# Rotation tables of the second to fourth layer made by GpSimd in place of VectorE

## The chip, the cores and the metric
One Trainium2 chip, one core, one launch of the whole program. The metric is the device time in microseconds, the median of several executions. The core has TensorE (PE, matmuls and transposes), VectorE (DVE), ScalarE (ACT), GpSimd (POOL) and SyncE (SP, which here only issues DMAs). Each engine works through its own list of instructions in order, and engines wait for one another on semaphores.

## The reference, cut to what matters
The input is 8 sequences of 256 tokens of 512 numbers. Four parts follow one another, each added to its input after a layer norm: a small four-layer stack, a gated feed-forward network whose weights are scaled by a low-rank product, an attention, and the same feed-forward network again. The change touches only the first part. Each of its four layers does, with 64 channels:

```
y = silu(layernorm(h, l1w, l1b))
r = abs(phazor); p = tanh(r) * exp(1j * angle(phazor))
prog = p ** arange(L)                      # a decaying rotation, per channel
y = real(causal convolution of y with prog + last_conv * prog * p)
h = h + y * scl
h = h + W2 @ silu(W1 @ layernorm(h) + b1) + b2
```

The convolution with powers of p is a linear recurrence z[t] = p z[t-1] + y[t].

## The kernel before, in words
The kernel is in three phases; the first holds the stack and the first feed-forward network, beside preparations for the attention. The tokens are cut into four blocks of 512 (`NBLK` = 4), and each block passes the stack as a stack of its own, s = 0 to 3; s = 0 is called the lead, because the feed-forward network of block 0 can begin only when it is through. Then the network runs over blocks 0 to 3, 14 weight chunks each (`gate`, `up`, `down`, matmuls in the helper of line 837), and stacks 1 to 3 are worked off between its matmuls on TensorE.

In a layer the phases of the recurrence are taken out by a rotation: the input is multiplied by cos and sin of the angle times t (`ur` on VectorE, line 1765, and `ui` on GpSimd, line 1270), two real scans with the decay rho run over time (`zr`, `zi`, line 1776), and the results are multiplied by the same tables again (`pr`, line 1780, `pi`, line 1273), possibly summed (`prs`, line 1784) and taken through a matmul (`conv`). Each norm in a stack has the steps `sq` (squares, ScalarE), `h` (VectorE), `var` (TensorE), `eps` (VectorE, line 1751), `rstd` (the inverse root, GpSimd, line 1262), `rtr` (TensorE) and `yn` (VectorE, line 1757).

The tables are `rot`, cos and sin for 4 layers and 256 times (`cosT`, `sinT`). They are made by doubling in eight levels (`LEVELS` = 8): level k makes the columns n to 2n, n = 2^k, from the columns 0 to n by a rotation through the angle of n steps. That angle's cos and sin (`turn`) are squared up level by level on GpSimd (`turns`, lines 1239 to 1245; the semaphore `rot_done` counts them). Layer 0's table is made on VectorE level by level (`tab0`, `dve_table`, lines 1631 and 1633). The tables of layers 1 to 3 are made on VectorE too (`tabs`, `dve_tables`): levels 0 to 4 for the three layers together in three instructions each (lines 1649, 1656, 1658), levels 5 to 7 (`TAB_EACH` = 5) layer by layer in two instructions each (lines 1649, 1652). Each instruction counts up `tabs_dve`; `ui` and `ur` of layers 1 to 3 wait for the count `TABS[l]`, and the first two silus of the network's gate (line 1317) for `TABS["all"]`, since the scratch memory `tab` is the memory of `gate`.

The order of every engine's list in phase 1 comes from a greedy planner (`Steps.ordered`) that runs when the program is built. A step has an engine, a cost in us, the steps it comes after and an urgency. Each result is ready for others 0.12 us after its end (`LAG`; 0.25 for TensorE, none between two TensorE steps). The planner always places the ready step that ranks first by

```
late = urgent > 0 and at < patient and e in need and at + us > need[e] + 0.1
rank = (late, at, urgent, number[k])
```

where `at` is the earliest start, `number` the place in which the step was added, and `need[e]` the earliest expected start on that engine of a step of the lead (urgency 0) all of whose predecessors have a known time. The steps at issue are added in this loop, after the tile norms (`ln`, and `inv` on GpSimd, cost 1.7, urgency 2 in blocks 1 and later):

```
for k in range(LEVELS):
    o.add(("turn", k, 0), "pool", 1.0 if k else 0.2, ..., 1)
    o.add(("tab0", k, 0), "dve", 0.42 + 0.002 * (1 << k), ..., 1)
    for l in range(1, DEPTH) if k >= TAB_EACH else (0,):
        o.add(("tabs", k, l), ...)
```

`inv` h of the first norm gives the row scales of two tiles (lines 1159, 1166, 1171), and the rows of stacks 1 to 3 wait for them.

Of the kernel before, what the change touches and what calls it, by code (L numbers as in the profile page):

```python
# [10 lines left out]
ALU = mybir.AluOpType  # L11
# [3 lines left out]
P = 128  # L15
# [7 lines left out]
DEPTH, DIM, DFF = 4, 64, 256  # L23
# [30 lines left out]
LEVELS = SEQ.bit_length() - 1  # L54
# [114 lines left out]
def hybrid_block(nc, x_in, win, vecs, b1, w1, w2, wout, bout, ffn_w, lr_long, lr_short, wqkv, wo, qk_w, out, weff_gu, weff_dn, weff_s, weff_q, weff_x):  # L169
    with ExitStack() as ctx:  # L170
# [33 lines left out]
        for phase in ("phase1", "phase2", "phase3"):  # L204
# [14 lines left out]

        const_done, zero_done, prep_dve, base_done, inv_abs, rho_in, rho_done, rot_done, tab0_dve, tabs_dve = (  # L220
            sem(n) for n in ("const_done", "zero_done", "prep_dve", "base_done", "inv_abs", "rho_in", "rho_done",
                             "rot_done", "tab0_dve", "tabs_dve"))
        fold_mm, fold_dve, fold_act, winc_done, scan0_done, lr_hi_done, lr_lo_done = (sem(n) for n in (
# [189 lines left out]
        def set_up_steps(o):  # L413
# [18 lines left out]
            for k in range(LEVELS):  # L432
                o.add(("turn", k, 0), "pool", 1.0 if k else 0.2, [("turn", k - 1, 0) if k else ("root", 0, 0)], 1)
                o.add(("tab0", k, 0), "dve", 0.42 + 0.002 * (1 << k), [("turn", k, 0)] + ([("tab0", k - 1, 0)] if k else []), 1)
                for l in range(1, DEPTH) if k >= TAB_EACH else (0,):
                    o.add(("tabs", k, l), "dve", 0.5 + 0.0025 * (2 << k) if l else 0.65 + 0.015 * (1 << k), [("turn", k, 0)] + (
                        [("tabs", k - 1, l if k > TAB_EACH else 0)] if k else []), 1 + l)
# [764 lines left out]
        def pool_positions():  # L1202
# [5 lines left out]
                      allow_small_or_imprecise_dtypes=True).then_inc(rel_done, 1)  # L1208

        def pool_phase1():  # L1210
            pool.memset(ident[:], 0.0).then_inc(const_done, 1)
# [36 lines left out]
            for what, a, b in order1["pool"]:  # L1248
# [5 lines left out]
                elif what == "turn":  # L1254
                    turns(a)
                elif what == "inv" and (a, b) == (1, 0):
                    pool_first_inverse()
# [6 lines left out]
                elif what == "ui":  # L1264
                    if b == 0:
                        pool.wait_ge(tab0_dve, TAB0)
                    else:
                        pool.wait_ge(tabs_dve, TABS[b])
                    pool.wait_ge(stk_act[a], ON_ACT[a]["silu", b])
# [24 lines left out]
        def act_ffn(what, a, b):  # L1294
# [277 lines left out]

        TAB0, TABS, n_made = 2 * LEVELS, {}, 0
        for _, k, l in (e for e in order1["dve"] if e[0] == "tabs"):
            n_made += 2 if l else 3
            TABS["all"] = n_made
            if k == LEVELS - 1:
                TABS[l] = n_made
        FOLD = counts(k for k in order1["dve"] if k[0] == "fold")
# [55 lines left out]

        def dve_tables(k, layer):

            n, ls = 1 << k, slice(layer, layer + 1) if layer else slice(1, DEPTH)
            nl = ls.stop - ls.start
            old, new, crossed = rot[:, :, ls, 0:n], rot[:, :, ls, n:2 * n], rot[:, ::-1, ls, 0:n]  # L1640
            ta = tab[:, 1, 0:2 * nl * n].rearrange("p (i l t) -> p i l t", i=2, l=nl)
            pair = turn[:, 0:2, k, ls].rearrange("p i (l o) -> p i l o", o=1).broadcast_to([P, 2, nl, n])
            done = n_tab[0]
            dve.wait_ge(rot_done, k + 1)
            if k == 0:
                dve.wait_ge(const_done, 12)
            if done:
                dve.wait_ge(tabs_dve, done)
            dve.tensor_tensor(ta, crossed, pair, ALU.mult).then_inc(tabs_dve, 1)
            if layer:  # L1650
                dve.wait_ge(tabs_dve, done + 1)
                dve.scalar_tensor_tensor(out=new, in0=old, scalar=turn[:, 2, k, layer:layer + 1], in1=ta, op0=ALU.mult,
                                         op1=ALU.add).then_inc(tabs_dve, 1)
            else:
                both = turn[:, 2, k, ls].rearrange("p (i l o) -> p i l o", i=1, o=1).broadcast_to([P, 2, nl, n])
                dve.tensor_tensor(new, old, both, ALU.mult).then_inc(tabs_dve, 1)
                dve.wait_ge(tabs_dve, done + 2)
                dve.tensor_tensor(new, new, ta, ALU.add).then_inc(tabs_dve, 1)
            n_tab[0] += 2 if layer else 3

        n_tab = [0]

        def dve_scan_start():
# [34 lines left out]
        def dve_phase1():  # L1698
            dve.memset(long_raw, 0.0).then_inc(zero_done, 1)
            step(dve.memset(sm[:], 0.0))  # L1700
            for what, a, b in order1["dve"]:
# [9 lines left out]
                elif what == "tab0":  # L1711
                    dve_table(a)
                elif what == "tabs":
                    dve_tables(a, b)
                elif what == "scan0":
# [43 lines left out]
                elif what == "ur":  # L1759
                    if b == 0:  # L1760
                        dve.wait_ge(tab0_dve, TAB0)
                    else:
                        dve.wait_ge(tabs_dve, TABS[b])
                    dve.wait_ge(stk_act[a], ON_ACT[a]["silu", b])
# [1373 lines left out]
```

## Time and profile before
| | |
|---|---|
| median of 3 executions | 2368.31 us (2368.25 to 2370.93) |
| profiled execution | 2372.38 us, its span 2371.1 us |
| busy PE | 2328.1 us, 98% |
| busy DVE | 1589.5 us, 67% |
| busy ACT | 1218.3 us, 51% |
| busy POOL | 838.5 us, 35% |
| chain of waits | PE 93%, DVE 2%, DMA, ACT and POOL 1% each |

Times within the profile are measured from the start of its span. The chain of waits is followed back from the last instruction; shares are of the span. In the 40 slices of the page (59 us each) PE is busy to 6 and 8 tenths in the first two and to 9 or more in all the others.

### The profile page before, as it was taken

The numbers are of one execution on the slowest core, as the hardware profiler recorded it, in microseconds if no ns is written. First come the engines' busy times: TensorE is split into PE (matmuls) and PEld (weight loads), VectorE is DVE, ScalarE is ACT, GpSimd is POOL, SyncE is SP. The second block draws the span as 40 slices with busy tenths as digits, with TensorE's granted clock in tenths as the row PEclk, the third lists the DMA queues.
The fourth block names the chain that finished last, engine by engine and source line by source line (L and its number), as shares of the span: only waits on it lengthen the run. The fifth ranks groups of instructions, "written<-read, shape, count | busy, mean of one in ns | idle before, by whom it ended". The sixth has DMA issues, their size and how long they took to land.

```text
span 2371.1 us, 40814 instructions
## 1 busy us (share of the span) xinstructions
PE 2328.1 (98%) x12672; PEld 2015.7 (85%) x12672; DVE 1589.5 (67%) x3900; ACT 1218.3 (51%) x3827; POOL 838.5 (35%) x1332
## 2 busy tenths in 40 slices
PE   6899999999999999999999999999999999999999
PEld 4577777888899999999999999999999988888887
DVE  7666664534277777777777777777777776565553
ACT  7543332233266666666666666766766661232212
POOL 5550443212034445444454554444544440010000
PEclk8899999999999999999999999999999999999999
DMA  4335567987831534536346346364362225565554
GB/s 144 105 144 199 203 237 281 346 342 280 314 125 63 236 145 164 231 139 233 147 150 235 124 157 244 131 231 165 137 249 92 95 70 204 189 219 195 189 192 160
DMA packets 92627, 444.84 MB, mean 188 GB/s; under 512 B 10168, under 2 KB 17336, under 8 KB 72704
## 3 DMA queue, kind: packets, MB, share of 16 engines
q1 hardware_dynamic: 91056, 440.78, 50.5%
q8 instruction: 106, 1.74, 0.3%
q10 hardware_dynamic: 1360, 1.46, 0.2%
q14 instruction: 105, 0.86, 0.1%
HBM read 342.59 MB, written 99.61 MB: 186 GB/s over the span
## 4 chain that ended last, share of the span: by engine, by line
PE 93%; DVE 2%; DMA 1%; ACT 1%; POOL 1%; issue 1%; SPq 0%; DVEq 0%; POOLq 0%; ACTq 0%
PE psum L837 80%; PE psum L2832 4%; PE psum L2786 2%; PE psum L2821 1%; PE psum L2822 1%; PE psum L2777 1%; POOL x L1292 0%; POOL srstd L1262 0%; DMA wD<-weff_dn 0%; DMA short_raw<-in_lr_short 0%; DMA weff_s<-short_st 0%; PE psum L1812 0%; PE psum L1981 0%; PE psum L1959 0%; PE psum L1971 0%
## 5 line engine op out<-in xcount | busy, mean ns | idle before, releaser
L837 PE MATMUL psum<-qw,xs 128*128 128x384 f32 x2688 | 548.6, 346 | 0.2 <-DVE su L2630 0.2
L837 PEld LDWEIGHTS psum<-qw,xs 128*128 128x128 f32 x2688 | 457.8, 188 | 1.0 <-issue 0.4
L2603 POOL TENSOR_SCALAR prob<-prob,rsum 128x128 f32<-128x128 f32 (+1 forms) x512 | 228.9, 460 | 527.3 <-DVE rsum L2711 527.2
L2545 ACT ACTIVATE prob<-biased,nmax 128x256 f32<-128x256 f32 (+1 forms) x512 | 227.2, 446 | 151.0 <-DVE nmax L2701 147.7
L2719 DVE TENSOR_TENSOR oT_l<-psum,oT_h 128x512 fp32r<-128x512 f32 x128 | 88.5, 692 | 193.9 <-ACT oT_h L2557 193.9
L837 PE MATMUL psum<-wo_h,oT_h 128*128 128x512 f32 x512 | 208.5, 407 | 0.0
L837 PE MATMUL psum<-wo_l,oT_h 128*128 128x512 f32 x512 | 203.5, 397 | 0.0
L837 PE MATMUL psum<-wo_h,oT_l 128*128 128x512 f32 x512 | 202.0, 394 | 0.0
L2486 ACT ACTIVATE squares<-cc 128x128 f32<-128x128 f32 x512 | 154.3, 305 | 41.0 <-DVE cc L2633 31.4
L2552 ACT ACTIVATE pT_h<-psum 128x384 fp32r<-128x384 f32 x256 | 125.2, 489 | 76.1 <-PE psum L2832 73.7
L2569 POOL TENSOR_TENSOR rr<-ss,mneg_half 128x6 f32<-128x6 f32 (+1 forms) x128 | 150.1, 1173 | 10.7
L837 PE MATMUL psum<-xT0h,wgu 128*128 128x512 f32 x448 | 151.2, 399 | 1.4 <-DVE svar L1751 1.4
L837 PE MATMUL psum<-xT1h,wgu 128*128 128x512 f32 x448 | 147.9, 395 | 0.0
L2714 DVE TENSOR_TENSOR pT_l<-psum,pT_h 128x384 fp32r<-128x384 f32 x256 | 141.7, 553 | 8.1 <-ACT pT_h L2552 1.8
L837 PE MATMUL psum<-xw_h,wS 128*128 128x512 f32 x448 | 147.0, 389 | 0.0
L2699 DVE SCALAR_TENSOR_TENSOR low_bias<-alibi,q_root,psum 128x128 f32<-128x128 f32 x256 | 88.4, 345 | 49.0 <-PE psum L2822 48.2
L2832 PE MATMUL psum<-ident,prob 128*128 128x128 f32 x768 | 116.8, 274 | 0.0
L837 PEld LDWEIGHTS psum<-wo_h,oT_l 128*128 128x128 f32 x512 | 96.1, 188 | 23.8
L837 PE MATMUL psum<-xw_h,wA 128*128 128x512 f32 x336 | 112.6, 389 | 0.0
L837 PEld LDWEIGHTS psum<-wo_h,oT_h 128*128 128x128 f32 x512 | 96.4, 188 | 17.1 <-DVE oT_l L2719 0.5
L837 PE MATMUL psum<-kT,qT_h 128*128 128x256 f32 x512 | 109.3, 295 | 0.0
L837 PEld LDWEIGHTS psum<-wo_l,oT_h 128*128 128x128 f32 x512 | 96.5, 189 | 14.2
(360 smaller groups left out, 5863.9 us busy)
## 6 DMA issues: line engine op xcount, KB each, us to landing
xs<-weff_x SPq DMA_DIRECT2D x62, 1792.0 KB, 7.9
wgu<-weff_gu SPq DMA_DIRECT2D x42, 1024.0 KB, 7.4
qw<-weff_q SPq DMA_DIRECT2D x56, 768.0 KB, 7.8
weff_q<-q_parts SPq DMA_DIRECT2D x84, 384.0 KB, 2.4
wD<-weff_dn SPq DMA_DIRECT2D x56, 512.0 KB, 4.8
wS<-weff_s SPq DMA_DIRECT2D x28, 1024.0 KB, 7.2
wdn<-weff_dn SPq DMA_DIRECT2D x42, 512.0 KB, 4.6
weff_gu<-wgu SPq DMA_DIRECT2D x14, 1024.0 KB, 4.0
```

Source lines behind the costliest of these rows:

```text
L837: ins = pe.matmul(out_ap, stat[a], mov[b], start=start and n == 0, stop=stop and n == last)
L2486: ins = act.activation(squares[:, first_place + hd, :], cc[:, tile, half, (hd + 1) * HD:(hd + 2) * HD], ACT.Square, accum_out=ss[:, n:n + 1])
L2545: act.activation(prob[:, b, lo:hi], biased[:, b % 2, lo:hi], ACT.Exp, bias=nmax[:, b, t:t + 1], scale=-1.0, accum_out=esum[:, b, t:t + 1]) ...
L2552: act.activation(pT[0][:, b % 2, :], psum[:, b, 0:SC], ACT.Copy).then_inc(pT_hi, 1)
L2569: pool.tensor_tensor(rr[:, part], ss[:, part], mneg_half[:, 0:part.stop - part.start], ALU.pow).then_inc(r_done if b else r_part, 1)
L2603: pool.tensor_scalar(prob[:, b, lo:hi], prob[:, b, lo:hi], rsum[:, b, t:t + 1], 1.0, ALU.mult, ALU.mult).then_inc(prob_done, 1)
L2699: dve.scalar_tensor_tensor(out=low_bias[:, b % 2, :], in0=alibi[:, b, 0:P], scalar=q_root[:, b:b + 1], in1=psum[:, b, SC:SC + P], op0=ALU. ...
L2714: dve.tensor_tensor(pT[1][:, b % 2, :], psum[:, b, 0:SC], pT[0][:, b % 2, :].bitcast(F32), ALU.subtract).then_inc(pT_lo, 1)
L2719: dve.tensor_tensor(oT[1][:, hs, :], psum[:, 2 * b, :].rearrange("p (h c) -> p h c", h=2), oT[0][:, hs, :].bitcast(F32), ALU.subtract).the ...
L2777: ins = pe.transpose(psum[:, across_bank(what, a, b), t * P:(t + 1) * P], cc[:, t, 0, 0:HD], ident[:])
L2786: ins = pe.transpose(psum[:, across_bank(what, a, b), hd * P:(hd + 1) * P], q_heads(b)[:, hd // 2, hd % 2, :], ident[:])
L2832: ins = pe.transpose(psum[:, b, k * P:(k + 1) * P], prob[:, b, k * P:(k + 1) * P], ident[:])
```

## The change
The steps `tabs` go from VectorE's list to GpSimd's, with other costs in the planner, and there is one form for all: three instructions a step (product with the crossed sines, product with the cosine, sum) instead of two for levels 5 to 7. The semaphore is renamed.

```
-                    o.add(("tabs", k, l), "dve", 0.5 + 0.0025 * (2 << k) if l else 0.65 + 0.015 * (1 << k), [("turn", k, 0)] + (
+                    o.add(("tabs", k, l), "pool", 0.6 + 0.005 * (2 << k) if l else 0.75 + 0.03 * (1 << k), [("turn", k, 0)] + (
                         [("tabs", k - 1, l if k > TAB_EACH else 0)] if k else []), 1 + l)
...
+        for _, k, l in (e for e in order1["pool"] if e[0] == "tabs"):
+            n_made += 3
...
+        def pool_tables(k, layer):
+
+            n, ls = 1 << k, slice(layer, layer + 1) if layer else slice(1, DEPTH)
+            nl = ls.stop - ls.start
+            old, new, crossed = rot[:, :, ls, 0:n], rot[:, :, ls, n:2 * n], rot[:, ::-1, ls, 0:n]
+            ta = tab[:, 1, 0:2 * nl * n].rearrange("p (i l t) -> p i l t", i=2, l=nl)
+            pair = turn[:, 0:2, k, ls].rearrange("p i (l o) -> p i l o", o=1).broadcast_to([P, 2, nl, n])
+            done = n_tab[0]
+            pool.wait_ge(rot_done, k + 1)
...
+            if done:
+                pool.wait_ge(tabs_done, done)
+            pool.tensor_tensor(ta, crossed, pair, ALU.mult).then_inc(tabs_done, 1)
+            both = turn[:, 2, k, ls].rearrange("p (i l o) -> p i l o", i=1, o=1).broadcast_to([P, 2, nl, n])
+            pool.tensor_tensor(new, old, both, ALU.mult).then_inc(tabs_done, 1)
+            pool.wait_ge(tabs_done, done + 2)
+            pool.tensor_tensor(new, new, ta, ALU.add).then_inc(tabs_done, 1)
...
+                elif what == "tabs":
+                    pool_tables(a, b)
...
-                        pool.wait_ge(tabs_dve, TABS[b])
+                        pool.wait_ge(tabs_done, TABS[b])
...
-                    act.wait_ge(tabs_dve, TABS["all"])
+                    act.wait_ge(tabs_done, TABS["all"])
...
-            if layer:
-                dve.wait_ge(tabs_dve, done + 1)
-                dve.scalar_tensor_tensor(out=new, in0=old, scalar=turn[:, 2, k, layer:layer + 1], in1=ta, op0=ALU.mult,
-                                         op1=ALU.add).then_inc(tabs_dve, 1)
```

## Rows read from the trace of the kernel before

**Rows 1.** The first line of the page.
```profile
span 2371.1 us, 40814 instructions
```
**Rows 2.** Stretches: length; busy PE, PEld, DVE, ACT, POOL; clock; DMA share; GB/s.
```profile
0.00:117.30 117.30, 85.13 (x502) 57.89 (x502) 86.37 (x219) 76.92 (x165) 59.76 (x115) 0.85 0.40 126
117.30:375.00 257.70, 253.80 (x1261) 194.82 (x1262) 168.54 (x280) 93.90 (x155) 94.81 (x104) 1.00 0.55 197
```
**Rows 3.** Waits of PE, 117 to 375 us: total us, times, longest.
```profile
PE psum L1944 <- DVE buf_c L1784: 2.9, 2, 1.9
PE psum L837 <- DVE svar L1751: 1.4, 1, 1.4
```
**Rows 4.** The stretch 34 to 102 us, columns as in rows 2.
```profile
34.00:102.00 68.00, 56.84 (x362) 39.82 (x363) 51.71 (x104) 49.66 (x106) 35.78 (x43) 0.88 0.32 105
```
**Rows 5.** Groups of DVE: out<-in xcount | busy us, mean ns | idle before.
```profile
L1652 DVE SCALAR_TENSOR_TENSOR rot<-rot,turn,gate 128x256 f32<-128x256 f32 x3 | 1.5, 485 | 0.1
...
L1649 DVE TENSOR_TENSOR gate<-rot,turn 128x64 f32<-128x64 f32 x3 | 0.7, 223 | 0.1
...
L1658 DVE TENSOR_TENSOR rot<-rot,gate 128x96 f32<-128x96 f32 x1 | 0.3, 258 | 0.0
...
L1656 DVE TENSOR_TENSOR rot<-rot,turn 128x96 f32<-128x96 f32 x1 | 0.2, 246 | 0.0
```
**Rows 6.** POOL in order of time: start us, us, instruction [idle before <-releaser].
```profile
16.51 0.25 POOL L1235 TENSOR_SCALAR turn<-turn 128x4 f32<-128x4 f32 x1 [3.13 <-DVE sm L1619]
...
18.09 0.20 POOL L1239 TENSOR_TENSOR sm<-turn 128x4 f32<-128x4 f32 x1
...
23.62 0.22 POOL L1245 TENSOR_SCALAR turn<-sm 128x4 f32<-128x4 f32 x1
25.15 1.18 POOL L1262 TENSOR_TENSOR srstd<-svar,mneg_half 128x4 f32<-128x4 f32 x1 [1.31 <-DVE svar L1751]
26.41 0.19 POOL L1159 TENSOR_SCALAR ln_var<-ln_sq 128x2 f32<-128x2 f32 x1
...
27.46 0.20 POOL L1171 TENSOR_TENSOR ln_nmr<-ln_nm,ln_rstd 128x2 f32<-128x2 f32 x1
...
44.97 1.51 POOL L1262 TENSOR_TENSOR srstd<-svar,mneg_half 128x4 f32<-128x4 f32 x1 [5.72 <-DVE svar L1751]
```
**Rows 7.** DVE in order of time, columns as in rows 6.
```profile
25.00 0.42 DVE L1631 TENSOR_TENSOR gate<-rot,turn 128x256 f32<-128x256 f32 x1
25.46 0.48 DVE L1633 SCALAR_TENSOR_TENSOR rot<-rot,turn,gate 128x256 f32<-128x256 f32 x1
...
28.88 0.42 DVE L1765 TENSOR_TENSOR buf_c<-buf_e,rot 128x256 f32<-128x256 f32 x1 [0.45 <-ACT buf_e L1450]
...
43.02 1.28 DVE L1726 TENSOR_TENSOR short_st<-short_raw,short_st 32x512 fp32r<-32x512 f32 x2
44.34 0.48 DVE L1740 TENSOR_SCALAR h<-psum,vec_c 128x256 f32<-128x256 f32 x1
...
48.60 0.43 DVE L1765 TENSOR_TENSOR buf_c<-buf_e,rot 128x256 f32<-128x256 f32 x1
```
**Rows 8.** ACT in order of time, columns as in rows 6.
```profile
28.18 0.60 ACT L1450 ACTIVATE buf_e<-buf_d,vec 128x256 f32<-128x256 f32 x1
...
42.96 0.47 ACT L1441 ACTIVATE buf_b<-psum,vec_c 128x256 f32<-128x256 f32 x1 [0.27 <-PE psum L1971]
```
**Rows 9.** A group of POOL, columns as in rows 5.
```profile
L1224 POOL TENSOR_TENSOR center<-center,ident 128x128 f32<-128x128 f32 x1 | 0.5, 454 | 0.1
```
**Rows 10.** Single lines over the span: ns min/median/max, first and last start.
```profile
L1270 POOL TENSOR_TENSOR buf_b<-buf_e,rot x16: 726/972/1731, 28.9 to 337.1; 128x256 f32<-128x256 f32 x16
...
L1262 POOL TENSOR_TENSOR srstd<-svar,mneg_half x36: 1002/1017/1929, 25.1 to 363.7; 128x4 f32<-128x4 f32 x36
...
L1780 DVE TENSOR_TENSOR buf_c<-buf_d,rot x16: 391/506/969, 31.0 to 340.8; 128x256 f32<-128x256 f32 x16
```
**Rows 11.** POOL and DVE at 64 us, in order of time, columns as in rows 6.
```profile
64.15 0.91 POOL L1273 TENSOR_TENSOR buf_b<-buf_a,rot 128x256 f32<-128x256 f32 x1
...
64.40 0.95 DVE L1780 TENSOR_TENSOR buf_c<-buf_d,rot 128x256 f32<-128x256 f32 x1
```

More of the change, by code:

```diff
@@ L218, in hybrid_block @@
         x_out = sem("x_out")
-        const_done, zero_done, prep_dve, base_done, inv_abs, rho_in, rho_done, rot_done, tab0_dve, tabs_dve = (
+        const_done, zero_done, prep_dve, base_done, inv_abs, rho_in, rho_done, rot_done, tab0_dve, tabs_done = (
             sem(n) for n in ("const_done", "zero_done", "prep_dve", "base_done", "inv_abs", "rho_in", "rho_done",
-                             "rot_done", "tab0_dve", "tabs_dve"))
+                             "rot_done", "tab0_dve", "tabs_done"))
         fold_mm, fold_dve, fold_act, winc_done, scan0_done, lr_hi_done, lr_lo_done = (sem(n) for n in (
@@ L1208, in pool_positions @@
                       allow_small_or_imprecise_dtypes=True).then_inc(rel_done, 1)
+        TAB0, TABS, n_made = 2 * LEVELS, {}, 0
+        for _, k, l in (e for e in order1["pool"] if e[0] == "tabs"):
+            n_made += 3
+            TABS["all"] = n_made
+            if k == LEVELS - 1:
+                TABS[l] = n_made
+        def pool_tables(k, layer):
[6 more added lines that the diff above has]
+            pool.wait_ge(rot_done, k + 1)
+            if k == 0:
+                pool.wait_ge(const_done, 12)
+            if done:
[5 more added lines that the diff above has]
+            pool.tensor_tensor(new, new, ta, ALU.add).then_inc(tabs_done, 1)
+            n_tab[0] += 3
+        n_tab = [0]
         def pool_phase1():
@@ L1571, in dve_ffn @@
                 dve.tensor_tensor(sums_lo, sums, sums_hi.bitcast(F32), ALU.subtract).then_inc(gu_lo, 1)
[L1573 to L1578, printed above, removed]
         FOLD = counts(k for k in order1["dve"] if k[0] == "fold")
@@ L1634, in dve_table @@
                                      op1=ALU.add).then_inc(tab0_dve, 1)
[L1636 to L1649, printed above, removed]
-            if layer:
-                dve.wait_ge(tabs_dve, done + 1)
-                dve.scalar_tensor_tensor(out=new, in0=old, scalar=turn[:, 2, k, layer:layer + 1], in1=ta, op0=ALU.mult,
-                                         op1=ALU.add).then_inc(tabs_dve, 1)
[L1654 to L1661, printed above, removed]
         def dve_scan_start():
@@ L1712, in dve_phase1 @@
                     dve_table(a)
-                elif what == "tabs":
-                    dve_tables(a, b)
                 elif what == "scan0":
@@ L1762, in dve_phase1 @@
                     else:
-                        dve.wait_ge(tabs_dve, TABS[b])
+                        dve.wait_ge(tabs_done, TABS[b])
                     dve.wait_ge(stk_act[a], ON_ACT[a]["silu", b])
```

## The prediction

> **What bounds the kernel now.** I read the stretches first. The page's span is 2371.1 us [rows 1]. Until 117.3 us, where the first expert-network matmul of L837 starts, TensorE is busy for 85.13 us; from there to 375 us it is busy for 253.80 of 257.70 us [rows 2]. After 117.3 the kernel is bound by TensorE's own work: its waits from 117 to 375 us, where the other stacks run, add up to some 5 us, the largest 2.9 us behind `prs` (L1784) and 1.4 us behind an `eps` [rows 3]. Before 117.3 it is bound by a chain: the lead stack (s = 0), whose steps go one after the other through all four engines. TensorE idles for 117.3 - 85.13 = 32.2 us there, and between 34 and 102 us it is busy for 56.84 of 68 us, the lead's work and filling from stacks 1 to 3 together [rows 4]. So a microsecond added to the lead chain moves the end by one microsecond, less what TensorE does for the other stacks meanwhile; a microsecond of VectorE time alone moves nothing. VectorE's table work is not small: six groups of three instructions for levels 5 to 7, 1.5 down to 0.7 us and 6.5 us together, and 15 small ones of 0.16 to 0.26 us, some 9.2 us in all [rows 5]. What counts is who stood behind it.
>
> **The lead's first rotation.** Layer 0's own table stays on VectorE. Its last level waits for the last `turn` on GpSimd. That ends at 23.62 + 0.22 = 23.84 [rows 6]; the table's last two instructions run at 25.00 and 25.46 and end at 25.94, and `ur` of layer 0 starts at 28.88 [rows 7], after ScalarE's silu (28.18 + 0.60 [rows 8]). The table is 2.9 us early. That slack is what the change may use up for nothing.
>
> **The new order on GpSimd.** The planner takes the ready step with the earliest start, then the lowest urgency number, then the first listed. `turn` k+1 and `tabs` k both become ready 0.12 after `turn` k, both have urgency 1, and `tabs` k is listed first. So each of levels 0 to 3 of the three-layer tables goes ahead of the next `turn`. `turn` 0 ends at 16.76 [rows 6]. In the planner's costs four rounds are 4 turns of 1.0, tables of 0.78 + 0.81 + 0.87 + 0.99 and some lags, 7.9 us after 16.8: `turn` 4 ends near 24.8. Level 4 (1.23) would end at 26.1, later than the lead's inverse root, due at 25.15, so it is held back behind it; `turn` 5 likewise. Behind the root come `tabs` 4 and `turn` 5; then the inverse of tiles 4 and 5 (`inv` 0,2) is ready 0.12 us before `turn` 6 and gets in; then `turn` 6, and in the 0.12 us gap after it `tabs` 5 of layer 1; only then `turn` 7.
>
> **Its price.** A `turn` round is (23.84 - 18.09) / 6 = 0.96 us [rows 6]. A GpSimd multiply or add takes 0.20 us for 4 elements (18.09 [rows 6]), 0.454 for 128 [rows 9] and 0.726 at best for 256 [rows 10], so about 0.19 + 0.0021 per element. Three instructions a step give 0.6, 0.63, 0.7, 0.85 and 1.15 us for levels 0 to 4 (6 to 96 elements), 0.95 for 64, 1.35 for 128 and 2.2 for 256; in all 3.9 + 3 x 4.5 = 17.4 us on GpSimd for 9.2 taken off VectorE. The chain: 16.8 + levels 0 to 3 (2.8) + four turns (3.8) = 23.4; wait for the root, which runs 25.15 to 26.33; `tabs` 4 1.2, `turn` 5 1.0, `inv` 0,2 1.25 (26.41 to 27.66 before [rows 6]), `turn` 6 1.0, `tabs` 5 0.95, `turn` 7 1.0: 32.7. The last level on VectorE takes another 1.0 (0.94 and a hop), so `ur` starts at 33.75 in place of 28.88: **+4.9 us** on the lead. No row shows GpSimd with these broadcast operands. Below: at VectorE's price for the same shapes, 0.25 an instruction for 64 and 96 elements [rows 5], `tabs` 4 and `tabs` 5 lose 0.7 and what stands before the root is taken up by the idle stretch there: +4.2. Above: at the ratio of the median `ui` to the fastest, 972 to 726 ns, they gain 0.7, +5.6; at the slowest, 1731 [rows 10], the root comes 2.1 late as well, +10. I take 4.9, nearest to the uncontended rows.
>
> Here the port matters. At 64.15 GpSimd's `pi` took 0.91 us and the VectorE multiply beside it, started at 64.40, took 0.95 [rows 11], against 0.391 at its best [rows 10]; the inverse root takes 1.002 to 1.929 us [rows 10], and 1.51 at 44.97, where a two-input VectorE subtraction (43.02, two of them) ran up to and a third beside it [rows 6, 7]. The Trainium skill, "SBUF — State Buffer", section "Who interferes with whom", says that a VectorE instruction with two SBUF inputs and a GpSimd one that reads SBUF take turns, the first holding the port to its end; this case's trace agrees (0.95 against 0.39). It speaks against the change: in its terms the last level of table 0 would stand behind up to two GpSimd products of 0.45 us, +5.8 in place of +4.9. I keep 4.9; the sum does not use it.
>
> **What the lead gets back.** VectorE starts `h` 0,2 at 44.34, after the low parts of the low-rank factors ended [rows 7]; its square on ScalarE was done at 42.96 + 0.47 = 43.43 [rows 8]. With 9.2 us off VectorE those are done earlier: 0.9 us back. The inverse root behind it, 1.51 us, would take 1.0 to 1.2: 0.3 us. But behind root 0,1 GpSimd now has most of 13.5 us of layer tables to place before layer 1's `ur`. The planner fits them ahead of root 0,2 by costs of 1.88 for level 7, where I count 2.2, and 1.24 for level 6 where I count 1.35; with the pending inverses and one bias row it fills that gap, and the root waits about 1 us behind them. Without that overrun nothing, if all of 13.5 us stood there 5. I take 1.0. Layer 1's table itself (level 7 of layer 1) is made well before `ur` 0,1, formerly at 48.60 [rows 7]; the others are needed a layer later each, so the added waits of `ui`, `ur` and the first gate silu cost nothing; behind `ui` on GpSimd only roots queue, which need its result anyway. No DMA moves; SyncE's queue is untouched. Removing work from VectorE's queue elsewhere gives nothing before 117.3, as the lead's other VectorE steps start when TensorE or ScalarE release them. Lead chain: 4.9 - 0.9 - 0.3 + 1.0 = **+4.7 us** at the first L837.
>
> **What TensorE makes of it.** In these 4.7 us it can do stacks 1 to 3. At the occupancy of [rows 4], 84%, that would be 3.9 us; but stack 1's rows wait for `inv` 0,2 and 0,3, which now stand behind tables too, and the weight chunks that can be scaled ahead of the first gate are limited by three slots (`WSLOTS`). Between 0 and 3.9 I take 1.3, a third, since the stacks are chains as well. Sum: 4.7 - 1.3 = **+3.4 us**. The profiled execution took 2372.38 (its span 2371.1 and 1.3 around it) and would take 2375.8; it lay 4.07 above the median of the three runs, 2368.31, which becomes **2371.7**.
>
> **Rivals.**
> - *Hidden.* The turns run ahead (GpSimd in fact takes them first), `turn` 7 ends before 27.8, and only the 1.2 us of relief and the 1.0 us of queueing remain: 0 +- 1.5, 2368.3. For it: 2.9 us of slack. Against: the rule of ties, which can be read in the code.
> - *GpSimd becomes the lead's bound in layer 1 too.* Every root after 0,1 stands behind tables of 2.2 us or, at contended prices (1.0 for 256 elements as `ui`'s median 972), 2.9: +3 on top of 4.9, less 1.2, less 1.3 filling: +6 to +8, 2375.5. For it: the filled gap. Against: after layer 1 GpSimd is half idle (35.78 of 68 us [rows 4]).
> - *Faster.* VectorE relief frees the lead of every late start there (1.2), and the replanned other stacks lose TensorE's waits behind `prs` and `eps` of 2.9 and 1.4 us [rows 3]; this decides if the turns aren't delayed by more than the slack. 1.2 + 4.3 = 5.5 less: 2362.8. Against: the work that those waits follow (bias rows on GpSimd, the later stacks' scans) is not touched by the change.
> - *Order noise.* Everything placed later in phase 1 is a new greedy order; a couple of microseconds either way around each case.
>
> **Chances.** Forecast 0.55, hidden 0.19, GpSimd bound 0.18, faster 0.08. A measurement tells 0.2%, 4.7 us. The forecast's case has its own range of 0 to +6.3 us (stall 4.2 to 6.5, the port included, less 0.2, filling 0 to 3.9), about a third of it beyond 4.7. So slower 0.55 x 0.33 + 0.17 = 0.35, faster 0.07, same 0.58. Range: from -1.8 (hidden, lower half) to +9.2 (GpSimd bound, upper end, and part of the slowest price, +10): 2366.5 to 2377.5.
>
> **What would show it.** Right: GpSimd's lines of `turn` and `tabs` alternate; the last `turn` ends near 32.7 rather than 23.84; `ur` 0,0 near 33.7; VectorE idle before it; `h` 0,2 starts straight after its square; the first L837 near 122; TensorE's busy time after it a microsecond or so shorter. Wrong: `turn` 7 before 27.8, or the first L837 within 1.5 us of 117.3, or an end that moves by more than the first L837 does. If tables of 256 elements take 2.2 us on GpSimd in isolation but 3 in place, the port is at work.

## The result, and the profile after

The changed kernel takes 2379.40 us (median of 6, 2377.27 to 2380.86) where the kernel before takes 2368.94 us beside it (median of 6, 2367.69 to 2376.11). The ratio, with its 95% interval, is 1.0038 [1.0027, 1.0049], some 9 us slower; the two medians themselves lie 10.5 us apart. The prediction said 2371.7 us, with a range up to 2377.5: too low, and outside the range. A second series gave 2379.48 us and 1.0036 [1.0024, 1.0048]. The profiled execution took 2380.86 us, its span 2379.6.

The page of the changed kernel, its span and busy times; they answer to [rows 1]:
```profile
span 2379.6 us, 40823 instructions
...
PE 2339.7 (98%) x12672; PEld 2024.5 (85%) x12672; DVE 1587.3 (67%) x3867; ACT 1218.2 (51%) x3827; POOL 858.1 (36%) x1374
```
The stretches of the changed kernel, with the columns of [rows 2]. The first three answer to [rows 2] and [rows 4]; the last is new:
```profile
0.00:117.30 117.30, 90.70 (x467) 61.73 (x467) 74.39 (x173) 70.41 (x149) 76.43 (x152) 0.90 0.41 126
117.30:375.00 257.70, 251.46 (x1254) 192.35 (x1253) 174.54 (x291) 96.98 (x168) 93.35 (x106) 0.98 0.51 184
...
34.00:102.00 68.00, 59.12 (x331) 41.57 (x329) 41.38 (x81) 46.62 (x101) 46.47 (x69) 0.90 0.32 105
90.00:130.00 40.00, 32.13 (x157) 20.21 (x158) 25.45 (x52) 16.28 (x34) 19.22 (x22) 0.70 0.00 1
```
The same last stretch of the kernel before, for comparison:
```profile
90.00:130.00 40.00, 33.41 (x192) 21.97 (x191) 22.43 (x47) 17.79 (x38) 25.26 (x24) 0.91 0.03 14
```
GpSimd is busy 16.7 us longer up to 117.3 (76.43 against 59.76) and VectorE 12.0 us shorter, but over the whole span VectorE is busy only 2.2 us less (1587.3 against 1589.5). `lr` below are VectorE's subtractions that make the low parts of the low-rank factors, and chunk 0 is the first of the network's weight chunks.

GpSimd of the changed kernel around the lead's first root, with the columns of [rows 6], which it answers to:
```profile
23.23 1.06 POOL L1270 TENSOR_SCALAR turn<-sm 128x4 f32<-128x4 f32 x1
24.25 1.07 POOL L1272 TENSOR_SCALAR turn<-sm 128x4 f32<-128x4 f32 x1
...
26.42 1.04 POOL L1292 TENSOR_TENSOR srstd<-svar,mneg_half 128x4 f32<-128x4 f32 x1 [0.92 <-DVE svar L1746]
27.43 0.35 POOL L1229 TENSOR_TENSOR gate<-rot,turn 128x96 f32<-128x96 f32 x1
...
29.17 0.73 POOL L1273 TENSOR_SCALAR turn<-sm 128x4 f32<-128x4 f32 x1
29.98 0.23 POOL L1159 TENSOR_SCALAR ln_var<-ln_sq 128x2 f32<-128x2 f32 x1
...
32.69 0.29 POOL L1229 TENSOR_TENSOR gate<-rot,turn 128x64 f32<-128x64 f32 x1
...
34.37 0.21 POOL L1273 TENSOR_SCALAR turn<-sm 128x4 f32<-128x4 f32 x1
```
VectorE of the changed kernel in the same time, answering to [rows 7]:
```profile
23.15 2.08 DVE L1717 TENSOR_TENSOR long_st<-long_raw,long_st 32x896 fp32r<-32x896 f32 x2 [1.88 <-ACT long_st L1430]
25.27 0.48 DVE L1729 TENSOR_SCALAR h<-psum,vec_c 128x256 f32<-128x256 f32 x1
...
35.47 0.69 DVE L1560 TENSOR_TENSOR stage<-stage,psum 128x512 f32<-128x512 f32 x1 [0.93 <-PE psum L1807]
36.08 0.42 DVE L1655 TENSOR_TENSOR gate<-rot,turn 128x256 f32<-128x256 f32 x1
36.53 0.48 DVE L1657 SCALAR_TENSOR_TENSOR rot<-rot,turn,gate 128x256 f32<-128x256 f32 x1
37.05 0.43 DVE L1760 TENSOR_TENSOR buf_c<-buf_e,rot 128x256 f32<-128x256 f32 x1
```
The reader sees the foreseen order: behind the root a table, a turn, the inverse, a turn, a table, the last turn. The last turn ends at 34.58 in place of 23.84, and `ur` of layer 0 starts at 37.05 in place of 28.88: +8.2 us. Two things were not foreseen. Turn instructions that take 0.2 us take 1.06 and 1.07 beside the subtractions of `lr` (23.15, two of about 1 us). And the last level of table 0, whose turn was done at 34.58, starts at 36.08, behind a product for weight chunk 0 that itself waited for TensorE (L1807).

TensorE of the changed kernel at the start of the network, answering to [rows 3] and to the first L837 at 117.28:
```profile
114.22 3.78 PE L1976 MATMUL psum<-wout_sb,buf_e 64*128 64x512 f32 x8
117.93 1.12 PE L1929 MATMUL psum<-ident,buf_b 128*128 128x128 f32 x4
121.71 2.08 PE L1954 MATMUL psum<-buf_e,w_sb 64*128 64x256 f32 x8 [2.66 <-DVE buf_d L1752]
123.86 3.48 PE L1823 MATMUL psum<-ident,xn 128*128 128x128 f32 x16
128.92 0.47 PE L837 MATMUL psum<-xT0h,wgu 128*128 128x512 f32 x1 [1.58 <-DVE xT0l L1553]
```
The first L837 of the kernel before:
```profile
117.28 0.47 PE L837 MATMUL psum<-xT0h,wgu 128*128 128x512 f32 x1 [1.42 <-DVE svar L1751]
```
The first L837 is 11.6 us late. From there to the end of the span are 2379.6 - 128.9 = 2250.7 us, against 2371.1 - 117.3 = 2253.8, so 3.1 us less are left. Of these, 1.3 us are TensorE's busy time (2241.7 against 2243.0) and 1.8 us its idle time (9.0 against 10.8). 11.6 - 3.1 = 8.5 us is the difference of the spans. Up to the first L837 TensorE is idle no longer than before (30.9 us against 32.2) but busy for 98.0 us in place of 85.1.

### The profile page after: what moved, and what is told of

Same layout as the page of the kernel before. It is cut to its first block, busy times and chain, and to the rows that moved or that the text cites. A ratio compares the mean times of both kernels' runs of the same rounds, so it can differ in the third digit from the quotient of the medians.

```text
span 2379.6 us, 40823 instructions
## 1 busy us (share of the span) xinstructions
PE 2339.7 (98%) x12672; PEld 2024.5 (85%) x12672; DVE 1587.3 (67%) x3867; ACT 1218.2 (51%) x3827; POOL 858.1 (36%) x1374
## 4 chain that ended last, share of the span: by engine, by line
PE 94%; DVE 2%; POOL 1%; DMA 1%; issue 1%; ACT 1%; SPq 0%; DVEq 0%; POOLq 0%; ACTq 0%
PE psum L837 81%; PE psum L2827 4%; PE psum L2781 2%; PE psum L2816 1%; PE psum L1954 1%; PE psum L2817 1%; PE psum L1966 1%; PE psum L2772 1%; DMA wD<-weff_dn 1%; PE psum L1807 1%; PE psum L1913 1%; PE psum L1976 0%; POOL srstd L1292 0%; DMA x<-in_x 0%; PE psum L1823 0%
## 5 line engine op out<-in xcount | busy, mean ns | idle before, releaser
L837 PE MATMUL psum<-qw,xs 128*128 128x384 f32 x2688 | 547.6, 346 | 0.2 <-DVE su L2625 0.2
L837 PEld LDWEIGHTS psum<-qw,xs 128*128 128x128 f32 x2688 | 456.8, 188 | 1.0 <-issue 0.4
L837 PE MATMUL psum<-wo_h,oT_h 128*128 128x512 f32 x512 | 208.2, 407 | 0.0
L837 PE MATMUL psum<-wo_l,oT_h 128*128 128x512 f32 x512 | 203.0, 396 | 0.0
L837 PE MATMUL psum<-wo_h,oT_l 128*128 128x512 f32 x512 | 202.4, 395 | 0.0
L2564 POOL TENSOR_TENSOR rr<-ss,mneg_half 128x6 f32<-128x6 f32 (+1 forms) x128 | 150.3, 1174 | 10.7
L837 PE MATMUL psum<-xT0h,wgu 128*128 128x512 f32 x448 | 152.6, 400 | 1.6 <-DVE xT0l L1553 1.6
L837 PE MATMUL psum<-xw_h,wS 128*128 128x512 f32 x448 | 147.0, 389 | 0.0
L837 PE MATMUL psum<-xT1h,wgu 128*128 128x512 f32 x448 | 145.6, 392 | 0.0
L837 PEld LDWEIGHTS psum<-wo_h,oT_l 128*128 128x128 f32 x512 | 96.1, 188 | 23.5
L837 PE MATMUL psum<-xw_h,wA 128*128 128x512 f32 x336 | 112.6, 389 | 0.0
L837 PEld LDWEIGHTS psum<-wo_h,oT_h 128*128 128x128 f32 x512 | 96.4, 188 | 16.9 <-DVE oT_l L2714 0.5
L837 PE MATMUL psum<-kT,qT_h 128*128 128x256 f32 x512 | 109.3, 295 | 0.0
L837 PEld LDWEIGHTS psum<-wo_l,oT_h 128*128 128x128 f32 x512 | 96.6, 189 | 14.5
```

The lines of the kernel that those rows point to most:

```text
L837: ins = pe.matmul(out_ap, stat[a], mov[b], start=start and n == 0, stop=stop and n == last)
L2564: pool.tensor_tensor(rr[:, part], ss[:, part], mneg_half[:, 0:part.stop - part.start], ALU.pow).then_inc(r_done if b else r_part, 1)
```

## The experiments

Times of this table are from the profiled executions, in us from the start of the span; the ratios are to the kernel before, timed beside it on the same chip. "Last turn" is the start of the last turn's last instruction, "`ur` 0,0" the start of `ur` of layer 0 of the lead, and "rest" the span from the first L837 (L838, L840 in some) on.

| kernel | last turn | `ur` 0,0 | first L837 | rest | ratio |
|---|---|---|---|---|---|
| before | 23.62 | 28.88 | 117.28 | 2253.8 | 1 |
| changed | 34.37 | 37.05 | 128.92 | 2250.7 | 1.0038 [1.0027, 1.0049] |
| e10 changed again | 33.41 | 36.31 | 127.95 | 2251.2 | 1.0036 [1.0024, 1.0048] |
| e12 other costs | 34.92 | 36.36 | 126.46 | 2251.9 | 1.0034 [1.0022, 1.0047] |
| e3 order only | 32.29 | 35.23 | 125.91 | 2251.3 | 1.0031 [1.0019, 1.0043] |
| e6 `lr` later | 32.55 | 33.99 | 125.81 | 2250.5 | 1.0029 [1.0020, 1.0038] |
| e5 small levels | 32.71 | 34.37 | 121.86 | 2250.2 | 1.0030 [1.0019, 1.0042] |
| e2 11 idle roots | 34.22 | 37.81 | 124.03 | 2256.0 | 1.0039 [1.0027, 1.0051] |
| e7 7 idle roots | 30.63 | 34.23 | 122.75 | 2251.2 | 1.0032 [1.0022, 1.0043] |
| e1 turns first | 24.27 | 29.68 | 122.71 | 2251.1 | 1.0016 [1.0008, 1.0025] |
| e4 large levels | 27.68 | 28.99 | 121.29 | 2248.9 | 1.0002 [0.9992, 1.0012] |
| e9 large, turns first | 23.57 | 29.42 | 121.55 | 2248.0 | 0.9999 [0.9990, 1.0008] |
| e8 cost + 0.1 | 23.09 | 29.90 | 118.18 | 2254.9 | 1.0024 [1.0011, 1.0037] |
| e11 cost - 0.05 | 23.37 | 29.77 | 122.61 | 2250.3 | 1.0005 [0.9996, 1.0014] |

**Is it the place of the turns?** The changed kernel with all table steps listed as ready only behind the last turn:
```
-  ("tabs", k, l), "pool", ..., [("turn", k, 0)] + ...
+  ("tabs", k, l), "pool", ..., [("turn", LEVELS - 1, 0)] + ...
```


> The changed kernel with one edit: in the planner the table steps come after the last turn instead of after their own, so that all eight turns go first on GpSimd; all tables are still made there (42 instructions). Theory A (the turn chain standing behind tables delays layer 0's rotation, and that delay is the loss): the last turn ends near 24, ur of layer 0 starts at 29 to 30.5 in place of 37.05, the first L837 at 117 to 120 in place of 128.92, and the time is 2367 to 2372, within 3 us of the kernel before. Theory B (GpSimd's 17 us of tables and its shared port are the loss wherever they stand): ur 0,0 is early too, but the roots of layer 1 wait behind tables, the first L837 comes at 122 or later and the time is 2374 to 2379. Theory C (any new greedy order costs this much): 2374 or more without a late first L837.

It gives back more than half: 1.0038 falls to 1.0016, 5.2 us. GpSimd does the same table work, but `ur` 0,0 starts at 29.68, as theory A said. The first L837 (122.71) and the time (2375.24) miss A's figures and lie in those of B, so this run alone does not decide between them: 3.8 us stay, and they arise behind the rotation. e11 below loses as much at the first L837 with VectorE making the tables.

The kernel before with its own order, in which 11 inverse roots whose result isn't read stand ahead of the last turn:
```
 def turns(k):
+    if k == LEVELS - 1:
+        for i in range(11):
+            pool.tensor_tensor(sm[:, 20 + i, :], ident[:, 0:DEPTH], mneg_half[:, 0:DEPTH], ALU.pow)
```


> The kernel before, its order of all five lists unchanged, with 11 inverse roots of 4 elements that nobody reads put on GpSimd ahead of the last turn (some 11 us, of which about 2.9 are slack): layer 0's rotation is late by 8 us with VectorE still making the tables and no new plan. Theory A: the first L837 some 8 us late or a little more, and the end 5 to 8 us later: 2374 to 2377. Theory C (the new order is the loss): with the old order TensorE makes most of it good and the end moves by less than 3 us.

`ur` 0,0 is 8.9 us late and the end is 9.2 us late by the ratio (8.9 by the spans), more than theory A's 5 to 8. In this order the lead's first root follows the last turn on GpSimd, and `ur` waits for the silu behind that root, not for the table:
```profile
34.40 1.03 POOL L1265 TENSOR_TENSOR srstd<-svar,mneg_half 128x4 f32<-128x4 f32 x1
```
```profile
37.81 0.43 DVE L1768 TENSOR_TENSOR buf_c<-buf_e,rot 128x256 f32<-128x256 f32 x1 [0.28 <-ACT buf_e L1453]
```
So the run shows what a late lead costs, whatever made it late; it does not test the table's own wait. The order is fixed and TensorE waits: it is idle for 39.7 us before the first L837, against 32.2. That matmul comes 6.8 us late, and another 2.2 us are added behind it. The waits of TensorE, 0 to 130 us, in this kernel (total us, times, longest):
```profile
PE psum L1931 <- POOL srstd L1265: 12.7, 4, 10.4
```
With 7 idle roots in place of 11:

> The kernel before, order unchanged, with 7 inverse roots that nobody reads ahead of the last turn instead of 11: 4 us less of stall, so layer 0's rotation is late by about 4.9 us, what the prediction gave to the change. With 11 of them the lead was 8.9 us late and the time 1.0039 of before. If the end follows the lead one to one where the order is fixed: ratio 1.002, 2375 to 2377. If a part is always made good: under 2374.

5.35 us at `ur` 0,0 cost 0.32%, 7.6 us, with an interval of 5.2 to 10.2 (by the spans 2.8; its profiled execution took 2375.23, its median is 2377.49). By the ratios of both runs a late lead is paid in full, or nearly; that it is paid more than in full is not shown.

**The order with less work.** All table instructions on two elements only, so that the rotations of layers 1 to 3 aren't computed (they are filled with 0.5), but stand where the change puts them:
```
+            ta, crossed, pair, old, new = (v[:, :, 0:1, 0:1] for v in (ta, crossed, pair, old, new))
...
+            both = both[:, :, 0:1, 0:1]
```


> The changed kernel with its order of all lists, but each table instruction works on 2 elements only, so that the tables of layers 1 to 3 are not made (their memory holds a constant 0.5 instead): order without most of the GpSimd work, about 42 x 0.2 = 8 us of it in place of 17. Theory A: the turns still stand behind the shortened tables and behind inv 0,2; ur 0,0 comes at 33 to 36, the end at 2374 to 2378. Theory B (load and port): most of the loss goes, under 2372. Theory C: 2377 or more, as the order is that of the changed kernel.

1.0031 of 1.0038: 7 of the 9 us stay, and the two intervals overlap. The size of the products accounts for little. But the 42 instructions still take 13.1 us in place of 18.4 (0.27 to 0.38 us each, where 8 us in all were expected), so this run does not separate the order from the number of instructions. The next two do.

**Which table steps?** Levels 5 to 7 alone on GpSimd, and levels 0 to 4 alone:
```
+                    mine = k >= TAB_EACH
+                    o.add(("tabs", k, l), "pool" if mine else "dve",
...
```
This is e4; e5 has `mine = k < TAB_EACH`. In both, VectorE's function for the tables is there again for the other levels.

> Half of the change: levels 0 to 4 of the tables (all three layers together) stay on VectorE in three instructions each, levels 5 to 7 (27 instructions, some 13.5 us) go to GpSimd. No table stands before turn 5; the last turn can be late by inv 0,2 and a table of 64 elements, to about 27. Theory A: ur 0,0 at 29 to 31, time within 3 us of before, 2366 to 2372. Theory B: 2374 or more, since three quarters of the GpSimd work and all its large instructions are there.

> The other half of the change: levels 0 to 4 of the tables go to GpSimd (15 small instructions, some 4 us), levels 5 to 7 stay on VectorE in two instructions each. The tables stand between the turns as in the changed kernel. Theory A (the turn chain): though only 4 us of GpSimd work moved, ur of layer 0 is late at 33 to 37, the first L837 at 123 to 128, the time 2375 to 2380. Theory B (load and port of the large tables): under 2373, since three quarters of the GpSimd work is gone.

The large levels cost 0.02%, within the noise, with 16.2 us of GpSimd work (the durations of their instructions added up); the small ones, with 5.4 us, cost 0.30%. They are the ones that the planner sets between the turns, and with them the last turn comes behind the lead's root and `inv` 0,2 as well. It is the place of the work that costs, not its amount. Of the two, e5's first L837 (121.86) came earlier than expected.

**The last 3 us at the rotation.** The changed kernel with the subtractions `lr` 2 and 3 planned behind the last level of table 0:
```
-                o.add(("lr", 2, piece), "dve", 1.0, [("lr", 0, 0)], 3)
+                o.add(("lr", 2, piece), "dve", 1.0, [("lr", 0, 0), ("tab0", LEVELS - 1, 0)], 3)
...
-                o.add(("lr", 3, piece), "dve", 0.6, [("lr", 1, 0)], 3)
+                o.add(("lr", 3, piece), "dve", 0.6, [("lr", 1, 0), ("tab0", LEVELS - 1, 0)], 3)
```


> The changed kernel with the low parts of the low-rank factors (VectorE subtractions with two SBUF inputs, 32 partitions, about 1.05 us each, and 0.68) planned after the last level of layer 0's table instead of beside the turns. In the changed kernel three turn instructions that take 0.2 us took 0.7 to 1.07 there, and the smul of weight chunk 0, which hangs on these factors, stood ahead of the last level. Theory P (port and queue on VectorE made the stall 8.2 instead of the 4.9 that the order alone gives): ur 0,0 at 33.5 to 34.5, the first L837 some 2 to 3 us earlier than 128.92, the time 2375 to 2378. If the stall is all in the order of GpSimd: ur stays near 36 to 37 and the time near 2379.

GpSimd and VectorE of this kernel:
```profile
32.55 0.21 POOL L1273 TENSOR_SCALAR turn<-sm 128x4 f32<-128x4 f32 x1
```
```profile
32.80 0.62 DVE L1655 TENSOR_TENSOR gate<-rot,turn 128x256 f32<-128x256 f32 x1 [1.04 <-POOL turn L1273]
33.45 0.50 DVE L1657 SCALAR_TENSOR_TENSOR rot<-rot,turn,gate 128x256 f32<-128x256 f32 x1
33.99 0.56 DVE L1760 TENSOR_TENSOR buf_c<-buf_e,rot 128x256 f32<-128x256 f32 x1
```
The last turn ends at 32.76 and `ur` starts at 33.99, where the prediction had 32.7 and 33.75. So the working of the order was right. In part the hit is luck: the root ends at 26.76, 0.4 us later than the 26.33 that was used, and the steps behind it take 6.0 us in place of 6.4. Most of the other 3 us come from what VectorE does beside the turns: it slows them and stands before the last table level. Some 0.8 us of them are not this: the next run, with nothing edited, has `ur` at 36.31. The ratio falls by 0.09% (2 us), which is less than the intervals can tell.

**Is 37.05 typical?** Nothing edited:

> The changed kernel once more, nothing edited. If its lateness is in the order that the program fixes, ur of layer 0 starts at 36 to 37.5 us again and the first L837 at 128 to 129.5. If the transfers that begin the program decide part of it (short_raw came 1.3 us later in its first profile), ur 0,0 starts at 34 to 36 and the first L837 1 to 3 us earlier than 128.92. Ratio to before 1.003 to 1.005 in either case.

36.31 and 127.95. In the first profile a transfer at the start of the program (`short_raw`) held ScalarE back by 1.15 us (its copy of `long_raw` starts at 21.42, here at 20.27), and the lead's first root came 0.75 us later (26.42 against 25.67). The instructions beside `lr` are slow again:
```profile
22.00 1.17 POOL L1273 TENSOR_SCALAR turn<-sm 128x4 f32<-128x4 f32 x1
23.26 0.96 POOL L1229 TENSOR_TENSOR gate<-rot,turn 128x48 f32<-128x48 f32 x1
```
**What does a new order alone do?** The kernel before, every instruction the same, with the planner's cost of the layer tables 0.1 us larger (e8, shown), and 0.05 us smaller (e11, 0.45 in place of 0.5):
```
-  "dve", 0.5 + 0.0025 * (2 << k) if l
+  "dve", 0.6 + 0.0025 * (2 << k) if l
```


> Control for theory C: the kernel before, its tables on VectorE, with the planner's cost of a layer table raised by 0.1 us. Work is the same, the greedy order of later steps differs. If a new order by itself costs: several us either way. Otherwise within 2.5 us of before, 2368 to 2374, with the first L837 near 117 to 118.

> The kernel before, in which only the planner's cost of the layer tables (levels 5 to 7) is 0.05 us smaller; every instruction is the same, the order is another one on all engines. It measures what a new order alone does. If a new order is noise around zero: within 0.1% of the kernel before, in either direction, against +0.24% for the order with a cost 0.1 us larger. If the kernel before is at a lucky order that any change loses: 1.001 to 1.003 slower again, with the first L837 within 2 us of 117.28.

The prediction priced this too low. The first L837 of e11:
```profile
122.61 0.47 PE L837 MATMUL psum<-xT0h,wgu 128*128 128x512 f32 x1 [1.50 <-DVE xT0l L1523]
```
The network begins 5.3 us late, though `ur` 0,0 is only 0.9 us late, and the rest is 3.5 us shorter: the end loses 1.2 us (1.0005, an interval that includes no change). In e8 the network begins on time and the end is 5.7 us late. The first L837 is no measure of the end: a new order moves work across that mark. And a new order alone can cost 0.24% [0.11%, 0.37%]. So no single ratio above proves a cause, as most of these kernels have an order of their own. Together they do: the eight rows whose `ur` 0,0 starts at 33.99 or later have ratios of 1.0029 to 1.0039, and the five with a change whose `ur` 0,0 starts at 29.90 or earlier have 0.9999 to 1.0024.

The changed kernel with other planner costs for the GpSimd steps (the turns stay between tables; the lead's first root now stands behind the table of level 4, later ones ahead of tables):
```
-  "pool", 0.6 + 0.005 * (2 << k) if l else 0.75 + 0.03 * (1 << k)
+  "pool", 0.9 + 0.0053 * (2 << k) if l else 0.6 + 0.0075 * (1 << k)
```


> The changed kernel with other planner costs of the GpSimd table steps (layer steps 0.9 + 0.0053 per column in place of 0.6 + 0.005, the common ones 0.6 + 0.0075 n in place of 0.75 + 0.03 n). The turns stay between tables, two roots of the lead come ahead of a table that they came behind, and TensorE's order differs in a few places. If the lateness at the rotation (+5 us by order) is what costs and the rest is order noise: ur 0,0 at 33.5 to 37, the first L837 at 122 to 127, ratio 1.001 to 1.0035. If what the lead loses behind the rotation belongs to GpSimd's table work itself: the first L837 at 128 or later and the ratio 1.004.

1.0034: with the rotation as late (36.36), the other order of roots and tables neither gives back nor costs anything that can be told.

**The best of both.** Levels 5 to 7 on GpSimd and behind the last turn (the edits of e4 and e1 together):

> Levels 0 to 4 of the tables stay on VectorE (three layers together, as before); levels 5 to 7 of layers 1 to 3 go to GpSimd and are listed after the last turn. Theory A (what costs is GpSimd's order ahead of the last turn): the last turn starts by 24.5 us (before 23.62, with levels 5 to 7 on GpSimd but not held back 27.68), ur of layer 0 at 29 to 30, the first L837 at 118 to 121, the end within 0.1% of the kernel before. Rival (the GpSimd table steps cost the lead at every layer, wherever they stand): ur 0,1 is 2 us or more late, the first L837 at 122 or later, the end 3 us or more above the kernel before.

0.9999: as fast as the kernel before, 0.37% below the changed one, and no gain from the VectorE time that it frees.

**Is it TensorE's clock?** From 90 to 130 us the granted clock reads 0.70 in the changed kernel and 0.91 before, a mean of stretches at 2.4 GHz and at 1.2, and the eight products with `w_sb` take 2.08 us at 121.71 and 1.13 us at 66.57. With the same 12672 matmuls TensorE is busy 9.1 us longer in e10 (2337.2 against 2328.1) and idle as long (41.9 against 43.0). So a theory stood open: the lowered clock as cause. The traces above already speak against it. In e2 the lead is as late, the end too, and the clock of this stretch reads 1.00:
```profile
90.00:130.00 40.00, 30.93 (x208) 20.87 (x207) 24.66 (x54) 19.44 (x43) 23.05 (x25) 1.00 0.05 20
```
TensorE is busy for 2328.6 us there and idle for 51.4, so nearly the whole loss is waiting. In e5, e6 and e7 the clock reads 0.91, as in the kernel before, and they lose 0.29 to 0.32%; in e4 and e9 it reads 0.83 and 0.87, and they lose nothing. A further test gives TensorE idle transposes (their result isn't read) after the lead's variances and identity products, 72 of them, mainly from 70 us on (8 take 1.04 us at full clock and 1.95 at half, so some 10 us in all), in the changed kernel and in the kernel before:
```
+        def extra(n):
+            for i in range(8):
+                pe.transpose(psum[:, OWN[n], (2 + i % 2) * P:(3 + i % 2) * P], ident[:], ident[:])
...
+                    if lead and b >= 4:
+                        extra(0)
...
+                    if lead and b >= 2:
+                        extra(0)
```
The first condition stands behind `var`, the second behind the identity products (`idc` and `idw`).

> The changed kernel with 72 idle 128x128 transposes on TensorE (their result isn't read): 8 behind each variance of the lead from the fifth on and 8 behind each identity product of h from the third layer on (56 to 72 of them between 70 and 120 us, some 0.14 us each at full speed, 10 us in all). Theory D (behind the late lead TensorE runs out of ready work between 90 and 130 us, its granted clock is 0.70 there against 0.91 before, so its matmuls take up to twice as long, and that is where +11.6 us of busy time come from): with the extra work the clock from 90 to 130 reads 0.85 or more, the 64x256 product with w_sb takes near 0.40 us each in place of 0.67, and the first L837 starts no later than 128, although there is 10 us more to do; the end at 2376 to 2380. Rival (the clock is a by-product, the lead's lateness and the order are the cost): the first L837 moves out by 3 us or more, the end by as much, to 2383 or later.

> The kernel before with the same 72 idle transposes. Its clock from 90 to 130 us is 0.91 as it is, so there is little to win: by both theories the first L837 is 1 to 5 us later than 117.28 and the end 1 to 6 us later than before. The difference between this cost and that of the run on the changed kernel is what the clock is worth: by theory D 3 us or more, by the rival about 0.

> The kernel with levels 5 to 7 on GpSimd behind the last turn (0.9999 of before) with the same 72 idle transposes. If the busier TensorE gives what it gave the kernel before (0.9987): clock from 90 to 130 us 0.95 or more in place of 0.87, the first L840 at 117 to 120 in place of 121.55, the end 2 to 5 us earlier, ratio 0.998 to 0.9992. If that gain was chance: ratio 1.000 to 1.002.

And 128 transposes, from the lead's second variance and first identity product on:

> The kernel before with 8 idle transposes behind every variance of the lead but the first and behind every identity product of h: 128, 56 of them more before 70 us, where the clock reads 0.66 from 20 to 50. If the clock can be had there too: the lead's idw of layer 0 (35.45) and idc of layer 1 (44.88) 1 to 3 us earlier, the first L837 at 114 to 116, ratio 0.997 to 0.9985. Rival: at half speed 8 transposes take 2.4 us and stand before the lead's own steps, so the lead loses 1 to 5 us there, ratio 0.9995 to 1.002.

> The changed kernel with the same 128 idle transposes. Theory D (the clock is part of its loss): half speed until 52 us gets shorter, the first L837 at 124 to 128 in place of 128, the end 1 to 4 us earlier than 2379.4 although TensorE has 18 us more to do. Rival (only GpSimd's order costs): first L837 at 129 or later, the end at 2380 or later.

| kernel | clock 90 to 130 | first L837 | TensorE busy | ratio |
|---|---|---|---|---|
| e13 changed, 72 | 0.79 | 130.45 | 2342.6 | 1.0034 [1.0021, 1.0046] |
| e14 before, 72 | 1.00 | 116.61 | 2330.1 | 0.9987 [0.9978, 0.9996] |
| e15 e9's kernel, 72 | 0.96 | 123.05 | 2328.3 | 1.0005 [0.9996, 1.0014] |
| e16 before, 128 | 0.96 | 122.62 | 2337.9 | 1.0020 [1.0010, 1.0030] |
| e18 changed, 128 | 0.89 | 132.96 | 2342.4 | 1.0057 [1.0043, 1.0071] |

The stretch 90 to 130 us of e15 and of e18:
```profile
90.00:130.00 40.00, 32.55 (x210) 22.49 (x206) 29.95 (x59) 19.14 (x41) 26.34 (x28) 0.96 0.00 1
```
```profile
90.00:130.00 40.00, 31.03 (x207) 21.82 (x208) 22.71 (x49) 16.61 (x36) 17.33 (x20) 0.89 0.00 1
```
The clock rises with the idle work, but the end doesn't follow the clock. In e18 it is 0.89, and the network begins 4 to 5 us later than without. The 128 transposes cost the changed kernel 0.21% and the kernel before 0.20%, though they raise the clock of this stretch by 0.19 in the one and by 0.05 in the other. The test is weaker than was meant: e13 reaches 0.79 where 0.85 was expected, and both in e13 and in e18 the eight products with `w_sb` right before the network still take 2.08 us, so the last stretch before the first L837 stayed slow. Some 10 us of added work cost the changed kernel nothing (1.0034 against 1.0036), so there was slack of that kind; a gain appears only in e14. With the rows of e2, e5, e6 and e7 the theory falls as the cause of the loss. That the slow matmuls of the changed kernel stand where TensorE would otherwise wait for the lead fits its idle time, but is argued, not shown. e14 is the one version measured faster than both kernels, by 0.13%; since the same edit gave e9's kernel 0.06% more time, I would not carry it over as a method. Why it helps there stays open.

## Why the prediction was wrong, point by point

- *What bounds the kernel.* Right. TensorE is idle for only 9.0 of 2250.7 us behind the first L837, and the lead sets the start.
- *The slack of 2.9 us.* Used as said: the last turn is 10.7 us late, `ur` 8.2.
- *The order on GpSimd and the +4.9.* The order was right to the instruction, and the sum also, with some luck: e6 gives 32.76 and 33.99 for 32.7 and 33.75. The step that failed is the choice in "I take 4.9, nearest to the uncontended rows". The run gave +8.2 (e10 +7.4), inside the bounds of 4.2 to 10. By rows: the last turn ends at 34.58, 1.9 later than 32.7 (e10: 0.9), through contention and a root 1.3 later, which comes in part from a late transfer at the start of this execution; level 7 of table 0 starts at 36.08, 1.3 later than its usual 0.2 behind the turn (e10: 1.5), behind chunk 0. The contention was seen in the working, but put in the wrong place: at the table on VectorE. The planner had moved the two-input subtractions of `lr` up into VectorE's freed time, right beside the turns. The Trainium skill, "SBUF — State Buffer", section "Who interferes with whom", says that a VectorE instruction with two SBUF inputs contends with a GpSimd instruction that reads SBUF. The rows agree (1.06 us in place of 0.19), for an instruction of only 4 elements.
- *GpSimd's prices.* Right for single instructions: 0.19 + 0.0021 per element gave 0.32, 0.39, 0.46 and 0.73 us for 64, 96, 128 and 256 elements; uncontended products took 0.29, 0.35, 0.40 and 0.61, the last sum of 256 0.72. In place, with contention, the 42 instructions took 18.4 us (6.4 + 6.4 + 5.6) for a forecast of 17.4; in e5 the 15 small ones took 5.4 for 3.9.
- *What the lead gets back, 0.2 in sum.* Right as far as layer 1: the identity product behind `h` of its second half starts at 61.80 against 54.05, so 8.2 has become 7.7. From there it loses again: 9.1 at layer 3's (100.81 against 91.69), 10.6 at `out`, 11.6 at L837. Over the whole way it loses 3.4 us more, 0.5 got back included, where the sum had -0.2. No step of the prediction had such a loss. e11 shows the same without any change of instructions (0.9 becomes 5.3), so a new order can do it. Which step of the order does it here stays open.
- *Filling, 1.3.* TensorE's busy time behind the first L837 is indeed 1.3 us shorter (2241.7 against 2243.0; in e10 0.4). Its idle time there is another 1.8 us shorter, which the sum did not have: 3.1 in all. The lead's further loss (+3.4 net) and this gain (-3.1) look like one exchange, as in e11 (+4.4, -3.5). Together they are +0.3 where the prediction had -0.2 - 1.3 = -1.5.
- *The sum of the spans.* 8.2 + 3.4 - 3.1 = 8.5 against 4.9 - 0.2 - 1.3 = 3.4: 3.3 us of the 5.1 us were lost at the rotation, 1.8 in the exchange. A further 2.6 us of the 7.7 between 2371.7 and 2379.40 is the subtraction of 4.07 us for the profiled execution before; the one after lay only 1.5 above its median.
- *The rivals.* Hidden: false, the turns did not run ahead. GpSimd as bound in layer 1: false as a mechanism, the lead gains up to there. Its price was also added up wrongly: 4.9 + 3 - 1.2 - 1.3 is 5.4, not 6 to 8. Faster: the wait behind `prs` is indeed gone, which fits the 1.8 us less of idle time. The 1.4 us behind `eps` was no wait of another stack: it stands right before the first L837 (117.28), and 1.6 us behind `xT0l` stand there now. A wait of 2.7 us behind `buf_d` is new, ahead of the first L837. Relief of VectorE earned nothing (e4, e9). Order noise: named, but priced at "a couple of microseconds"; e8 shows 5.7. It was left out of the sum, though it can be larger than the forecast's own 3.4.

## What to carry to other kernels

Here work taken off an engine that isn't late earned nothing, and on the new engine its place in the queue counted more than its length: 5.4 us between the steps of a dependent chain (e5) cost 7 us, 16.2 us behind that chain (e9) cost nothing that could be measured. Where a greedy planner orders the program, first look at what it moves into the freed time (here the subtractions that share the port), and take the effect of a new order as a term of the sum, measured on a control whose instructions are the same (here 0.05% and 0.24%). A milestone halfway is only a measure of the end if the work behind it is the same.

## What the runs showed of the hardware that wasn't expected

- A GpSimd instruction of 4 elements a partition takes 1.06 and 1.07 us beside a VectorE subtraction of 896 (two in 2.08 us) on 32 partitions, 0.19 to 0.22 alone: the loss is the length of the neighbour, not its own.
- In the changed kernel the granted clock reads 1.00 from 20 to 50 us, but its products take about twice their time there (16 projections with `win_c` at 19.43 take 3.68 us, 16 of them at 110.72 before 1.95). In e10, the same program, the clock reads 0.50 to 0.67 in that time. By the durations, then, the engine of the first profile was at the lower level there, whatever the reading.
- Idle transposes raise the granted clock (0.91 to 1.00 before, 0.70 to 0.89 changed), and 72 of them, some 10 us, cost at most 0.06% in three kernels; 128 cost 0.2% in two.
